# Values projected from split latents and split weights, two pairs of heads at a time

## The reference

```
latent_kv = x @ w_kv_down                    # (8, 1024, 128)
kv = latent_kv @ w_kv_up                     # (8, 1024, 2 * 1024)
k, v = (kv[..., :HD], kv[..., HD:])
q = (x @ w_q).reshape(Bx, Tx, N_HEAD, HEAD_SIZE)
att = jnp.einsum('bqhd,bkhd->bhqk', q, k) * scale
att = jnp.where(causal, att, -jnp.inf)
att = jax.nn.softmax(att, axis=-1)
y = jnp.einsum('bhqk,bkhd->bqhd', att, v)
return y.reshape(Bx, Tx, HD) @ w_out
...
x = _layernorm(x + attention(x)); x = _layernorm(x + experts(x))
```

## Time and profile before

| what | us |
|---|---|
| median of 3 runs | 3114.01 |
| lowest and highest | 3110.05 and 3117.75 |
| span of the profiled execution | 3111.9 |
| TensorE busy in it | 2989.7 (96%) |
| VectorE, ScalarE, GpSimd busy | 2065.0, 1916.0, 1542.5 |

### The profile page before, as it was taken

One profiled execution on the slowest core, in us unless ns is written; L12 is line 12 of the kernel. 1 busy time (PEld: TensorE's weight loads), 2 busy tenths in 40 slices (PEclk: granted clock), 3 DMA queues, 4 the chain that ended last, 5 costly groups with the idle time before them and its releaser, 6 DMA issues. The chain is left out here.

```text
span 3111.9 us, 61721 instructions
## 1 busy us (share of the span) xinstructions
PE 2989.7 (96%) x19244; PEld 2385.4 (77%) x19244; DVE 2065.0 (66%) x5938; ACT 1916.0 (62%) x4173; POOL 1542.5 (50%) x1623
## 2 busy tenths in 40 slices
PE   8999999999999999999999999979989999999996
PEld 6666767767676766676766767669989999999996
DVE  6666767767666766676766767644968865445446
ACT  6676777767677767676776767645544444444443
POOL 4443444444443444344444444437767776666665
PEclk9999999999999999999999999989999999999998
DMA  7776777777777777687778777668734544434425
GB/s 176 201 198 182 203 207 187 197 207 189 198 200 195 192 201 201 184 202 207 187 197 206 185 206 195 172 234 283 252 116 101 130 108 102 98 87 91 109 49 164
DMA packets 397577, 544.57 MB, mean 175 GB/s; under 512 B 79528, under 2 KB 295976, under 8 KB 397248
## 3 DMA queue, kind: packets, MB, share of 16 engines
q1 hardware_dynamic: 355200, 490.05, 57.9%
q0 software_dynamic: 25152, 33.75, 6.5%
q10 hardware_dynamic: 16896, 16.78, 1.5%
HBM read 213.16 MB, written 159.47 MB: 120 GB/s over the span
## 5 line engine op out<-in xcount | busy, mean ns | idle before, releaser
L263 POOL TENSOR_SCALAR prob<-prob,inv 128x128 f32<-128x128 f32 (+7 forms) x1024 | 772.2, 754 | 1188.1 <-DVE inv L716 1181.1
L711 DVE CUSTOM_DVE_ANT_0 s_ps<-s_ps,mask 128x128 f32<-128x128 f32 (+7 forms) x1024 | 775.9, 758 | 530.0 <-PE s_ps L426 521.0
L603 ACT ACTIVATE prob<-s_ps,neg_max 128x128 f32<-128x128 f32 (+7 forms) x1024 | 760.5, 743 | 240.3 <-DVE neg_max L711 232.7
L435 PE MATMUL t_ps<-ident,prob 128*128 128x128 f32 x3328 | 537.1, 274 | 6.3 <-POOL prob L263 6.3
L435 PEld LDWEIGHTS t_ps<-ident,prob 128*128 128x128 f32 x3328 | 395.0, 140 | 50.1 <-POOL prob L263 8.6
L695 ACT ACTIVATE prob_t<-t_ps 128x512 f32<-128x512 f32 x512 | 306.1, 598 | 196.2 <-PE t_ps L435 196.1
L425 PE MATMUL s_ps<-k_hh,q_hl 128*128 128x512 f32 (+3 forms) x768 | 296.3, 386 | 32.5 <-ACT prob L603 32.4
L425 PE MATMUL s_ps<-w_lo,w_hi 128*128 128x512 f32 (+3 forms) x768 | 295.5, 386 | 21.2 <-ACT prob L603 20.2
L1760 PE MATMUL e_y<-w_hi,hid_hi 128*128 128x256 f32 (+1 forms) x1088 | 312.1, 287 | 0.0
L1761 PE MATMUL e_y<-w_lo,hid_hi 128*128 128x256 f32 (+1 forms) x1088 | 308.2, 283 | 0.0
L1762 PE MATMUL e_y<-w_hi,hid_lo 128*128 128x256 f32 (+1 forms) x1088 | 308.1, 283 | 0.0
(11 more groups left out here) (261 smaller groups left out, 6615.8 us busy)
## 6 DMA issues: line engine op xcount, KB each, us to landing
k_hh<-k_high SPq DMA_DIRECT2D x128, 256.0 KB, 4.6
s_d<-squares SPq DMA_DIRECT2D x64, 512.0 KB, 3.0
y_d<-c_res SPq DMA_DIRECT2D x128, 256.0 KB, 3.6
late_t<-s_d SPq DMA_DIRECT2D x256, 128.0 KB, 3.4
k_lz<-k_low SPq DMA_DIRECT2D x126, 256.0 KB, 5.4
w_lo<-k_high SPq DMA_DIRECT2D x124, 256.0 KB, 4.5
c_yt<-y_d SPq DMA_DIRECT2D x60, 512.0 KB, 7.1
s_d<-squares SPq DMA_DIRECT2D x64, 384.0 KB, 2.6
```

The costliest lines, as they stand in the source:

```text
L263: pool.tensor_scalar(pr, pr, inv[:, s % 4:s % 4 + 1], 1.0, ALU.mult, ALU.mult).then_inc(norm_done, 1)
L435: mm = pe.transpose(t_ps[s % 2][:, to * P:(to + 1) * P], prob[s % 4][:, j * P:(j + 1) * P], ident[:])
L603: act.activation(prob[s % 4][:, 0:(q + 1) * P], s_ps[s % 2][:, 0:(q + 1) * P], ACT.Exp, scale=-1.0, bias=neg_max[:, s % 4:s % 4 + 1], accu ...
L711: dve.tensor_tensor_reduce(part, part, mask[:, T - (q + 1) * P:T], 1.0, -MASKED, ALU.add, ALU.min, neg_max[:, s % 4:s % 4 + 1]).then_inc(m ...
```

## The change

Values are projected from `lat_hi`, `lat_lo` and split weights `wv_hi`, `wv_lo`, as three products that accumulate. One product has 256 columns, the value weights of two neighbouring pairs (n even and n+1). The even pair's call makes tokens 0 to 511 of both pairs, the odd pair's call tokens 512 to 1023 of both. Since pairs now hold values for longer, the values lie in two rings, `v_first` (3 deep) and `v_last` (2 deep). The value weights of both pairs are split with the weights of the odd pair. The whole fp32 latents are gone: ScalarE writes `lat_hi` straight from the PSUM bank, and VectorE subtracts from that bank. So the bank is free for the queries only once VectorE has read it, and `latents_copied` waits for `l_low` instead of `l_step`.

```diff
-        wv = [sb(f"wv{u}", [P, P]) for u in range(2)]
+        wv = sb("wv", [P, 2, P])
+        wv_hi, wv_lo = (sb(n, [P, 2 * P], F32R) for n in ("wv_hi", "wv_lo"))
...
-        v = [sb(f"v{u}", [P, QT, P]) for u in range(2)]
+
+        v_first = sb("v_first", [P, 3, 4, P])
+        v_last = sb("v_last", [P, 2, 4, P])
...
+        def values(n, k):
+            return v_first[:, n % 3, k, :] if k < 4 else v_last[:, n % 2, k - 4, :]
...
             def weights_low(n, u):
                 pool.wait_ge(w_high, n + 1)
                 pool.sem_inc(passed, 1)
-                pool.tensor_tensor(wqk_lo[u][:], wqk[u][:], wqk_hi[u][:].bitcast(F32), ALU.subtract).then_inc(w_low, 1)
+                low = pool.tensor_tensor(wqk_lo[u][:], wqk[u][:], wqk_hi[u][:].bitcast(F32), ALU.subtract)
+                if n % 2:
+                    low = pool.tensor_tensor(wv_lo[:], wv[:].rearrange("p u c -> p (u c)"), wv_hi[:].bitcast(F32),
+                                             ALU.subtract)
+                low.then_inc(w_low, 1)
...
                 if 4 in tiles:
+                    pe.wait_ge(v_copied, 2 * (n | 1) + 2)
...
             def latents_copied(b, c):
-                pe.wait_ge(l_step, 4 * b + 2 * c + 1)
+                pe.wait_ge(l_low, 2 * b + c + 1)
...
             def project_v(n, u, c):
+
                 first = isinstance(n, int) and n == 0
                 if c == 0:
-                    pe.wait_ge(w_in[u], 48 * (n >> 1) + 48)
-                    pe.wait_ge(l_step, 4 * (n >> 3) + 3)
+                    pe.wait_ge(w_low, (n | 1) + 1)
+                    pe.wait_ge(l_low, 2 * (n >> 3) + 2)
...
-                for j in range(4):
-                    k = 4 * c + j
-                    mm = pe.matmul(bank(n, c)[:, j * P:(j + 1) * P], lat[:, k * P:(k + 1) * P], wv[u][:],
-                                   start=True, stop=True)
+                for j in range(2):
+                    k = 4 * (n % 2) + 2 * c + j
+                    out, cols = bank(n, c)[:, 2 * j * P:2 * (j + 1) * P], slice(k * P, (k + 1) * P)
+                    pe.matmul(out, lat_hi[:, cols], wv_hi[:], start=True, stop=False)
+                    pe.matmul(out, lat_hi[:, cols], wv_lo[:], start=False, stop=False)
+                    mm = pe.matmul(out, lat_lo[:, cols], wv_hi[:], start=False, stop=True)
...
             def copy_v(n, u, c):
                 act.wait_ge(proj_done, 6 * n + 5 + c)
-                act.activation(v[u][:, 4 * c:4 * c + 4, :], bank(n, c).rearrange("p (j c) -> p j c", c=P),
-                               ACT.Copy).then_inc(v_copied, 1)
+                made, tiles = bank(n, c).rearrange("p (j r c) -> p r j c", r=2, c=P), slice(2 * c, 2 * c + 2)
+                if n % 2:
+                    act.wait_ge(pv_done[1], n)
+                    act.activation(v_last[:, :, tiles, :], made, ACT.Copy).then_inc(v_copied, 1)
+                elif n % 3 < 2:
+                    act.activation(v_first[:, n % 3:n % 3 + 2, tiles, :], made, ACT.Copy).then_inc(v_copied, 1)
+                else:
+                    act.activation(v_first[:, 2, tiles, :], made[:, 0, :, :], ACT.Copy)
+                    act.activation(v_first[:, 0, tiles, :], made[:, 1, :, :], ACT.Copy).then_inc(v_copied, 1)
...
-                act.activation(wqk_hi[u][:], wqk[u][:], ACT.Copy).then_inc(w_high, 1)
+                high = act.activation(wqk_hi[u][:], wqk[u][:], ACT.Copy)
+                if n % 2:
+                    high = act.activation(wv_hi[:], wv[:].rearrange("p u c -> p (u c)"), ACT.Copy)
+                high.then_inc(w_high, 1)
...
-                act.activation(lat[:, halves(i)], bank(b, i), ACT.Copy).then_inc(l_step, 1)
-                act.wait_ge(l_step, 4 * b + 2 * i + 1)
-                act.activation(lat_hi[:, halves(i)], lat[:, halves(i)], ACT.Copy).then_inc(l_step, 1)
+                act.activation(lat_hi[:, halves(i)], bank(b, i), ACT.Copy).then_inc(l_step, 1)
...
-                dve.wait_ge(l_step, 4 * b + 2 * i + 2)
-                dve.tensor_tensor(lat_lo[:, halves(i)], lat[:, halves(i)], lat_hi[:, halves(i)].bitcast(F32),
+                dve.wait_ge(l_step, 2 * b + i + 1)
+                dve.tensor_tensor(lat_lo[:, halves(i)], bank(b, i), lat_hi[:, halves(i)].bitcast(F32),
                                   ALU.subtract).then_inc(l_low, 1)
```

More of the change, by code:

```diff
@@ L79, in attention_stage @@
         xt, xt_hi, xt_lo = R.xt, R.xt_hi, R.xt_lo
-        lat = sb("b_lat", [P, T])
         wd_hi = sb("wd_hi", [P, KC, RANK], F32R)
@@ L293, in load_weights @@
                 sp.dma_start(wqk[u][:, KC, :], w_k[:, bass.ds(m * P, P)]).then_inc(w_in[u], 16)
-                sp.dma_start(wv[u][:], w_v[:, bass.ds(m * P, P)]).then_inc(w_in[u], 16)
+                sp.dma_start(wv[:, u, :], w_v[:, bass.ds(m * P, P)]).then_inc(w_in[u], 16)
             def load_x(b):
@@ L457, in pv @@
                             keys = late_row(h, k - 4)
-                        mm = pe.matmul(o_ps[64 * h:64 * h + 64, off:HALF], v[u][:, k, 64 * h:64 * h + 64], keys,
+                        mm = pe.matmul(o_ps[64 * h:64 * h + 64, off:HALF], values(n, k)[:, 64 * h:64 * h + 64], keys,
                                        start=(k == 0), stop=(k == 4 * g + 3), skip_group_check=True)
@@ L622, in weights_high @@
                 if not (isinstance(n, int) and n < 2):
-                    act.wait_ge(proj_done, 6 * n - 8)
-                act.activation(wqk_hi[u][:], wqk[u][:], ACT.Copy).then_inc(w_high, 1)
+                    act.wait_ge(proj_done, 6 * n - (6 if n % 2 else 8))
+                high = act.activation(wqk_hi[u][:], wqk[u][:], ACT.Copy)
+                if n % 2:
+                    high = act.activation(wv_hi[:], wv[:].rearrange("p u c -> p (u c)"), ACT.Copy)
+                high.then_inc(w_high, 1)
             def x_split(b, i):
```

## The result

The changed kernel takes 3146.19 us as the median of 4 runs (3140.33 to 3150.99), the kernel before 3112.78 beside it (3110.05 to 3117.75). The ratio is 1.0107, with a 95% interval of 1.0092 to 1.0122: slower by 33 us, clear of noise. The forecast was 3142, the range 3124 to 3158. The profiled execution is the 3150.99 us one, the slowest of the four, with a span of 3149.2; so its trace has 37.3 us to account for, not 33.

The account below looks back on a forecast made before the run. TensorE, busy 96% of the span, was taken as nearly always the bound. The terms -9.0 + 0 + 1 + 9 + 27.3 gave +28 us on the 3111.9 span, 3140; with the median 2.1 above, 3142, range 3124 to 3158.

Parts of the forecast that it names:

- The value products: Value blocks of slots 8 and 10 on TensorE: six 256-column matmuls replace 8 records; 9.0 us gained in all.
- Slot 8: Value block on TensorE falls from 0.90 to 0.72 us: 0.18 saved in 50 pairs, 9.0 us gained.
- Slot 10: Loop of scores, maximum and exp ends last, so the second saving turns into a wait: 0 gained.
- The split of the value weights: GpSimd's added subtraction delays slot 7's transposes by 0.28 us in 31 odd pairs: 9 us lost.
- The copies of the values: ScalarE's copies stay single activations except in 11 even pairs, with two of half size: 1 us taken for all.
- Fresh latents: Queries wait for VectorE's subtraction in pairs m = 6: 2.41 us in slot 12, 1.49 in slot 15, 27.3 lost over 7 batches.
- rival (b): Clock falls in the new slot 12 stalls, 1.8 us each, 13 us more if every one does: 3155; chance 0.17.
- The DMA pairs: In 13 of 63 pairs a squares' DMA ends later anyway and swallows slot 8's 0.18 us saving.
- (a): Rival: weights' split hides, GpSimd's delay taken up by TensorE's lateness in slots 5 and 6: +19, 3133; chance 0.22.
- (c): Rival: fresh waits mostly given back, 1 us a batch staying of 3.9: +8, 3122; chance 0.09.
- (d): Rival: faster; fresh wait costs nothing and value products save in both slots: -10, 3104; chance 0.06.

Follow-up runs that it names:

- e4: Changed kernel with two more value products of 256 columns in slot 10 of each of 63 pairs; 3149.29 us, ratio 1.0102 to the kernel before.
- e5: Changed kernel with two more value products of 256 columns in slot 8 instead of slot 10; 3163.54 us, ratio 1.0159 to the kernel before.
- e1: Kernel before with one line changed: fresh queries wait for VectorE's subtraction of the latents instead of ScalarE's copy; 3155.14 us, ratio 1.0125.
- e2: Changed kernel with VectorE's subtraction of the latents put ahead of the maximum in slots 12 and 15; 3123.68 us, ratio 1.0023 to the kernel before.
- e9: Changed kernel with value weights split in slot 7 and whole fp32 latents kept in an idle half of x's buffer; 3112.10 us, ratio 0.9991.
- e8: Changed kernel with the latents' subtraction ahead of the maximum and the value weights split in slot 7; 3115.07 us, ratio 0.9998 to the kernel before.

## Why the prediction was right, point by point

**The value products.** Slot 8 saved 0.19 us in the rows read and 0.18 in every undisturbed pair, as forecast from the experts' products. Slot 10 saved nothing on top of it; e4 and e5 show that TensorE has slack there and none in slot 8. That the loop of scores, maximum and exp ends last in slot 10 is read from the rows, where the scores begin 0.05 us behind the end of exp.

**The split of the value weights.** The mechanism was right and the size a little low: 0.34 us instead of 0.28, 10.5 us instead of 9. The transposes of slot 7 begin 0.28 us later, as forecast: 1.09 us behind the scores L434 at 1031.38, where it was 0.81 (1012.58 to 1013.39). Left out of the sum was that the next products now begin 0.59 us behind these transposes instead of 0.53 (1032.47 to 1033.06, before 1013.39 to 1013.92). ScalarE's part cost nothing on top.

**The copies of the values** cost nothing where 1 us was taken: the 11 pairs in which a copy is made in two halves are as long as the other pairs of their place, 30.52 or 30.53 us, and 30.68 and 30.70 in two pairs m = 5.

**Fresh latents.** 3.95 us a batch against 3.90. e1 shows that the wait alone does it, e2 that it is the place in VectorE's stream and not the subtraction. Nothing gave the time back. With one operand in PSUM the subtraction takes 0.65 us beside a running L268 of GpSimd, with two in SBUF 1.47, in the kernel before as in e1 and e9. The rule on the shared port that the prediction cites from the Trainium skill (SBUF — State Buffer, section "SBUF: two separate sides") agrees with these rows.

**The clock**, rival (b), was left out of the sum. It came true in 4 of 7 batches of the profiled run, 1.6 us each against 1.8 taken, and in two more of the DMA pairs than before, which the prediction did not think of. Without the clock's 6.4 and 3.1 us the profiled run has 27.8 us to explain, and the forecast had 28. That they meet so closely is in part luck: the products saved 11.2 instead of 9.0, the copies cost 0 instead of 1, the weights 10.5 instead of 9, the latents 27.7 instead of 27.3, and these misses of up to 2 us cancel to 1.3.

**The DMA pairs.** The forecast let 13 pairs swallow 0.18 us each. The trace shows these pairs growing, by 3.1 us in all, about what two more falls of the clock cost. e8 and e9 agree: a faster chain was given back there in good part, in e9 5 of 11 us in the pairs of the profiled execution, and 8 of 11 by the times of all runs. This step of the prediction was too mild, and it did not decide the result. Whether a faster chain makes the falls more frequent or they only scatter (0 to 4 of 7 pairs m = 4 from run to run) is open.

The rivals (a), (c) and (d) fall: the weights' split showed in full, and the waits in full.

## What to carry to other kernels

When an edit lets a later reader, not an earlier one, free a buffer, price it by that reader's place in its engine's stream: here 1.7 of 2.5 us were instructions queued ahead of a 0.65 us subtraction, and moving it in front of them brought 19 us back in the pairs and the clock's falls in slot 12 besides, 25 us by the times. Ask of each saved matmul whether the next instruction of its engine can start earlier: of two equal savings, one was worth 0.18 us a pair and the other nothing. And a kernel with a DMA wait of its own may give back what was saved elsewhere; cut that transfer in a test run to see the saving itself.

## What was not expected of the hardware

At the end of the stall of slot 12, 2.3 us without a matmul, the granted clock fell to the lower level in 4 of 7 batches of the profiled run, from the same code and nearly the same times, and in 16 of 35 over the five profiled executions with this stall. It did not fall once at the 1.5 us stall of slot 15, nor in slot 12 with 1.8 us of it filled. When it falls, it costs 1.6 us there. But the length of a single gap is not what decides: behind the waits for the squares it also fell after a longest gap between matmuls of 1.0 us (174 us in the kernel before, where TensorE was busy 1.61 of 3 us). In the pairs m = 4 such a fall tells every pair over 34 us from the others.
